# Macaron layer with mixture-of-experts on one Trainium2 core: routing weights leave the sorted rows, and the third pool is sorted in one part

## The reference

```
x = x + 0.5 * ffn(layernorm(x))
x = x + attention(layernorm(x))      # causal, 16 heads, 4 key/value heads, width 128, rotary embedding
x = x + 0.5 * ffn(layernorm(x))

def ffn(x):                          # 16 experts of width 96, the best 2 for each token
    probs = softmax(x @ router_w)
    w, idx = top_k(probs, 2);  w = w / sum(w)
    y[e] = (silu(x @ gate_w[e]) * (x @ up_w[e])) @ down_w[e]
    return sum over the two chosen experts of w * y[e]
```

## Time and profile before

| | us |
|---|---|
| median of 3 runs | 965.21 (961.5 to 966.19) |
| the profiled execution | 959.92, its span 958.1 |
| busy in the span: PE, DVE, ACT, POOL | 817.7, 653.4, 572.4, 449.1 |
| L1547 and L1554, scatters | 32 and 32 |
| L1573 and L1568, gathers | 32 and 32 |
| L1227, evacuations | 124 |

### The profile page before, as it was taken

One profiled execution on the slowest core, in us unless ns is written; L12 is line 12 of the kernel. 1 busy time (PEld: TensorE's weight loads), 2 busy tenths in 40 slices (PEclk: granted clock), 3 DMA queues, 4 the chain that ended last, 5 costly groups with the idle time before them and its releaser, 6 DMA issues.

```text
span 958.1 us, 16817 instructions
## 1 busy us (share of the span) xinstructions
PE 817.7 (85%) x4840; PEld 689.6 (72%) x4840; DVE 653.4 (68%) x1592; ACT 572.4 (60%) x1536; POOL 449.1 (47%) x410
## 2 busy tenths in 40 slices
PE   4648999798999999999999999999996958989480
PEld 3637877677878788787888888787775837768370
DVE  5814665477787778788878788867789836565153
ACT  3314756686777677776787776876664624445140
POOL 1571233486586667563564563544434570030623
PEclk9977999999999999999999999999999979999785
DMA  9356983211011102000000000000000452465544
GB/s 296 122 182 180 270 225 114 73 18 21 7 17 18 17 1 28 8 1 1 1 1 2 1 1 1 2 2 7 1 1 1 171 159 63 128 185 174 162 136 153
DMA packets 52952, 70.73 MB, mean 74 GB/s; under 512 B 7552, under 2 KB 44672, under 8 KB 52480
## 3 DMA queue, kind: packets, MB, share of 16 engines
q1 hardware_dynamic: 40768, 47.61, 16.2%
q0 software_dynamic: 9216, 16.82, 7.1%
q10 hardware_dynamic: 2880, 5.24, 1.8%
HBM read 42.61 MB, written 27.03 MB: 73 GB/s over the span
## 4 chain that ended last, share of the span: by engine, by line
PE 52%; issue 16%; POOL 13%; DVE 9%; DMA 4%; ACT 3%; another core or an unknown queue 2%; ACTq 0%; DVEq 0%; SPq 0%; POOLq 0%
PE ps L1637 43%; PE ps L1833 4%; POOL sb_x L1573 3%; POOL sb_ropeB L1582 3%; POOL sb_xf L1585 3%; PE ps L1691 2%; POOL sb_wF L1593 1%; POOL xs L1554 1%; DMA sb_x<-ys,sb_pos 1%; PE ps L1705 1%; DVE sb_x L1433 1%; DVE sb_nmax L1406 1%; DVE sb_wF L1413 1%; POOL xs L1547 1%
## 5 line engine op out<-in xcount | busy, mean ns | idle before, releaser
L1637 PE MATMUL ps<-sb_wF 128*128 128x512 f32 (+2 forms) x1056 | 283.4, 391 | 21.0 <-issue 9.2
L1637 PEld LDWEIGHTS ps<-sb_wF 128*128 128x128 f32 x1056 | 173.1, 195 | 35.6 <-issue 14.9
L1582 POOL TENSOR_TENSOR sb_ropeB<-sb_ropeB,sb_sin 128x512 f32<-128x512 f32 x80 | 109.5, 1369 | 147.7 <-ACT sb_ropeB L951 147.7
L971 ACT ACTIVATE sb_prob<-ps,sb_nmax 128x128 f32<-128x128 f32 (+3 forms) x256 | 134.3, 526 | 65.4 <-DVE sb_nmax L1406 61.7
L1637 PE MATMUL ps<-sb_wF,sb_wA 128*128 128x512 f32 x576 | 155.4, 405 | 7.1 <-ACT sb_ropeB L951 5.9
L1406 DVE TENSOR_REDUCE sb_nmax<-ps 128x1 f32<-128x128 f32 (+3 forms) x256 | 122.2, 485 | 55.7 <-PE ps L1637 49.3
L1593 POOL TENSOR_TENSOR sb_wF<-sb_xf,sb_wF 128x384 fp32r<-128x384 f32 (+1 forms) x75 | 85.5, 1140 | 119.2 <-ACT sb_wF L963 119.2
L1433 DVE SCALAR_TENSOR_TENSOR sb_x<-ps,sb_rinv,sb_x 128x256 f32<-128x256 f32 x256 | 122.7, 479 | 25.6 <-PE ps L1637 10.6
L1413 DVE TENSOR_TENSOR sb_wF<-ps,sb_wF 128x512 fp32r<-128x512 f32 x160 | 109.5, 684 | 34.3 <-ACT sb_wF L980 29.9
L1637 PE MATMUL ps<-sb_wA,sb_wF 128*128 128x256 f32 x768 | 118.5, 292 | 13.9 <-DVE sb_x L1433 13.7
L1637 PEld LDWEIGHTS ps<-sb_wA,sb_wF 128*128 128x128 f32 x768 | 109.5, 195 | 24.5 <-issue 16.6
(11 more groups left out here) (200 smaller groups left out, 1348.9 us busy)
## 6 DMA issues: line engine op xcount, KB each, us to landing
ys<-sb_wA_raw SPq DMA_DIRECT2D x124, 128.0 KB
sb_wF_raw<-xs SPq DMA_DIRECT2D x44, 128.5 KB
sb_wA_raw<-xs SPq DMA_DIRECT2D x44, 128.5 KB
sb_work<-xs SPq DMA_DIRECT2D x36, 128.5 KB
sb_wA_raw<-in_wattn ACTq DMA_DIRECT2D x18, 256.0 KB, 3.9
sb_wF_raw<-in_wgu SPq DMA_DIRECT2D x4, 768.0 KB, 10.0
sb_wF_raw<-in_wdn SPq DMA_DIRECT2D x4, 768.0 KB, 16.7
sb_wA_raw<-in_wgu SPq DMA_DIRECT2D x4, 768.0 KB
```

The lines of the kernel that those rows point to most:

```text
L971: nc.scalar.activation(prob[k % 2][:, h, 0:(i + 1) * P], ps[:, bank_of((k * G + h) % (UB * G)), 0:(i + 1) * P], ACT.Exp, bias=nmax[:, k % ...
L1582: nc.gpsimd.tensor_tensor(ropeB[:, slot], ropeB[:, slot], sin[:], ALU.mult).then_inc(rope_mul, 1)
L1637: return nc.tensor.matmul(out, lhsT, rhs, start=start, stop=stop)
```

## The change

Rows have 256 numbers. The weights of both choices stay in SBUF (`wgt` has two planes). Both scatters of a token tile are issued from the same untouched row, all first choices ahead of all second ones, with no copy and no wait between them. `evacuate` is a plain copy. `shares` comes after `places` in each pool. The first ffn's gathers become plain transfers into four slots (rows of pool 0 for the first 8, `work` for the others), and DVE adds each with `scalar_tensor_tensor` (x = y * weight + x), at places of its own in `first_norm` and in the groups; the same instruction takes the place of L1313 in the second ffn. The norm of batch 0 comes two steps later in `first_norm`. The third pool's routing is one part over 12 token tiles, its logits and choices stand in groups 0 and 1, its places in group 2, and of its 24 scatters 9 stand in POOL's group 2 and 15 at the head of group 3.

```diff
-    RW = D + 1
-    xs = [nc.dram_tensor(f"xs{n}", (pools[n].pairs + P, RW), F32) for n in range(2)]
+    xs = [nc.dram_tensor(f"xs{n}", (pools[n].pairs + P, D), F32) for n in range(2)]
-    RING, XR, FR, GR = 8, 10, 4, 16
+    RING, XR, AR, GR = 8, 10, 4, 16
-    LN_FIRST = {5: (0,), 6: (1,), 7: (2, 3), 9: (5, 6), 10: (7,)}
+    LN_FIRST = {6: (0,), 7: (1, 2), 8: (3,), 9: (5, 6), 10: (7,)}
-    GATHERS = {(0, 1): range(12, 16), (0, 2): range(16, 20), (0, 3): range(20, 26), (1, 1): range(26, 32)}
+    GATHERS = {(0, 1): range(12, 16), (0, 3): range(16, 20), (0, 4): range(20, 24), (1, 3): range(24, 28),
+               (1, 4): range(28, 32)}
+    RESULTS_AT = {1: (0.0, 0.3, 0.3, 0.5), 3: (0.25, 0.6, 0.6, 1.0), 4: (0.0, 0.4, 0.4, 0.9)}
...
-                items = spread(items, [("gather", 0, j) for j in GATHERS[b, g]], 0.0, 0.5 if g == 1 else 1.0)
+                items = spread(items, [("gather", 0, j) for j in GATHERS[b, g]], *RESULTS_AT[g][0:2])
+            if (b, g) in GATHERS and engine == "dve":
+                items = spread(items, [("result", 0, j) for j in GATHERS[b, g]], *RESULTS_AT[g][2:4])
...
-        "act": {0: [(0.05, 0.4, range(8))], 1: [(0.2, 0.4, range(12, 16))]},
-        "dve": {0: [(0.76, 0.86, range(2)), (0.9, 1.0, range(2, 4))],
-                1: [(0.04, 0.1, range(4, 6)), (0.4, 1.0, range(12, 18))],
-                2: [(0.02, 0.4, range(18, 25)), (0.7, 0.9, range(26, 29))]},
-        "pool": {3: [(0.0, 0.0, range(12 + SECOND))]},
+        "act": {0: [(0.05, 0.4, range(8))], 1: [(0.0, 0.2, range(12, 16))]},
+        "dve": {0: [(0.7, 0.76, range(2)), (0.78, 0.82, range(2, 4)), (0.92, 0.96, range(4, 6))],
+                1: [(0.52, 0.98, range(12, 19))], 2: [(0.22, 0.5, range(20, 24))]},
+        "pool": {2: [(0.3, 1.0, range(9))], 3: [(0.0, 0.0, range(9, 2 * MT))]},
...
         def shares(q):
             dve.wait_ge(gtanh_done, q.p + 1)
-            tanh = gap(q, 1)
-            step(nc.vector.tensor_scalar(row_weights(q), tanh, 0.25, 0.25, ALU.mult, ALU.add))
-            nc.vector.tensor_scalar(wgt[:, q.t0:q.t0 + q.nt], tanh, -0.25, 0.25, ALU.mult, ALU.add)\
-              .then_inc(weight_done, 1)
-            settle()
+            for k, half in enumerate((0.25, -0.25)):
+                link(nc.vector.tensor_scalar(wgt[:, k, q.t0:q.t0 + q.nt], gap(q, 1), half, 0.25, ALU.mult, ALU.add))
+
+        def weighted_add(t, k, y):
+            return nc.vector.scalar_tensor_tensor(x[:, t // T, t % T], y, wgt[:, k, t:t + 1], x[:, t // T, t % T], ALU.mult,
+                                                  ALU.add)
+        def result(j):
+            t, k = pair(0, j)
+            dve.wait_ge(res_in[j % AR], 16 * (j // AR + 1))
+            if k == 1:
+                dve.wait_ge(res_done, j)
+            weighted_add(t, k, result_at(j)).then_inc(res_done, 1)
...
-            nc.vector.tensor_scalar(yo(s), y_at(s), tile_at(q, s)[:, D:D + 1], None, ALU.mult).then_inc(y_evac, 1)
+            nc.vector.tensor_copy(yo(s), y_at(s)).then_inc(y_evac, 1)
...
         def first_norm(i):
-            if 12 <= i < 12 + T:
-                dve.wait_ge(acc_in[i - 12], accumulated(1))
+            if 6 <= i < 6 + 2 * T:
+                result(i - 6)
+            if 14 <= i < 14 + T:
+                dve.wait_ge(res_done, T + i - 13)
...
-            elif i in (20, 21):
+            elif i in (21, 22):
...
-            elif n < 18:
-                chosen[q.p] = (0, 2 * T)
+            elif n < 19:
                 route(q, n - 12)
-                del chosen[q.p]
-            elif n < 24:
-                chosen[q.p] = (2 * T, q.nt)
-                route(q, n - 18)
-                del chosen[q.p]
...
         def scatter(q, n):
-            at = q.tokens + n
+            k, t = divmod(n, q.nt)
             if n == 0:
-                pool.wait_ge(weight_done, q.p + 1)
                 pool.wait_ge(to_done, q.p + 1)
...
+            nc.gpsimd.indirect_dma_start(out=xs[q.p][:], out_offset=place_of(q, k, t), in_=row(q, t),
+                                         in_offset=None).then_inc(scattered[q.p], 16)
...
-            nc.gpsimd.indirect_dma_start(out=x[:, t // T, t % T], out_offset=None, in_=ys[q.p][:], in_offset=where,
-                                         compute_op=ALU.add).then_inc(acc_in[t], 16)
+            if j >= AR:
+                pool.wait_ge(res_done, j - AR + 1)
+            if j % (2 * T) == 0 and j >= 4 * T:
+                pool.wait_ge(proj_done, normed(j // (2 * T) - 1))
+            nc.gpsimd.indirect_dma_start(out=result_at(j), out_offset=None, in_=ys[q.p][:],
+                                         in_offset=where).then_inc(res_in[j % AR], 16)
...
-        do(0, head_of("dve"))
+        do(0, spread(head_of("dve"), [("result", 0, j) for j in range(2 * T, 3 * T)], 0.5, 1.0))
```

More of the change, by code:

```diff
@@ L111, in program @@
         C = routing(own, "C")
-        rowC = sb("rowC", [P, MT, RW], F32, own)
+        rowC = sb("rowC", [P, MT, D], F32, own)
         C.update(placing(own, "C"))
@@ L213, in program @@
     y_out = [sem(f"y_out{r}") for r in range(RING)]
-    acc_in = [sem(f"acc_in{t}") for t in range(N)]
+    res_in = [sem(f"res_in{r}") for r in range(AR)]
+    res_done = sem("res_done")
     gat_in = [sem(f"gat_in{r}") for r in range(GR)]
@@ L352, in counts_of, with normed @@
         return counts or [JB[i] * b + v for i, v in enumerate(task_count(k, col))]
+    def normed(b):
+        n = max(n for n, (k, c) in enumerate(order) if c < 0)
+        return G + 3 + (b - 1) * JB[0] + n + 1
     def values_use(g):
@@ L437, in tile_at @@
         if r >= 7:
-            return work[:, (r - 7) * RW:(r - 6) * RW]
+            return work[:, (r - 7) * D:(r - 6) * D]
         flat, base = ((wF_flat, 20 * 512), (wA_flat, 27 * 512))[q.n]
-        return flat[:, base + r * RW:base + (r + 1) * RW]
+        return flat[:, base + r * D:base + (r + 1) * D]
     def rows_of(q):
@@ L593, in turn_of @@
                 items = third_pool(engine, g - KV, items)
+                if engine == "pool":
+                    items = spread(items, [("power", 0, 2 * B)], 0.8, 0.85)
             out += items
         return out
-    SECOND = 3
     EARLY_ROWS = 8
@@ L706, in gathers_of, with result_at @@
         return range(2 * q.t0, 2 * (q.t0 + q.nt))
-    def accumulated(k):
-        return 16 * (k + 1)
+    def result_at(j):
+        return (row(pools[0], j % AR) if j < 2 * T else work[:, (j % AR) * D:(j % AR + 1) * D])
     ADD_FROM = 7
@@ L1278, in last_pool @@
                 route(q, i - 10)
-            elif i == 18:
+            elif 18 <= i < 23:
+                places(q, i - 18)
+            elif i == 23:
                 shares(q)
-                places(q, 0)
-            elif 19 <= i < 23:
-                places(q, i - 18)
         def experts(n):
@@ L1312, in gather_add @@
                 dve.wait_ge(gadd_done, j)
-            nc.vector.tensor_tensor(xs_t, xs_t, gathered(j), ALU.add).then_inc(gadd_done, 1)
+            weighted_add(t, k, gathered(j)).then_inc(gadd_done, 1)
         def third(n):
@@ L1455, in do @@
                     early_norm(k, n)
+                elif what == "result":
+                    result(n)
                 elif n < 2:
                     if n == 0:
-                        for t in range(T):
-                            dve.wait_ge(acc_in[(b + 1) * T + t], accumulated(1))
+                        dve.wait_ge(res_done, 2 * T * (b + 2))
                     norm_stats(stats, b + 1, 2 * n, 2 * n)
@@ L1505, in _ @@
             route(pools[0], part)
-        shares(pools[0])
         for part in range(5):
             places(pools[0], part)
+        shares(pools[0])
         second_choices(0, 2 * FIRST_HALVES)
@@ L1511, in _ @@
         route(pools[1], 6)
-        shares(pools[1])
         for part in range(5):
             places(pools[1], part)
+        shares(pools[1])
         experts(0)
-        do(0, head_of("dve"))
+        do(0, spread(head_of("dve"), [("result", 0, j) for j in range(2 * T, 3 * T)], 0.5, 1.0))
         for b in range(B - 1):
@@ L1613, in _ @@
         for q in pools[0:2]:
-            for n in range(q.nt + SECOND):
+            for n in range(2 * q.nt):
                 scatter(q, n)
@@ L1626, in _ @@
         power(*NORMS[2 * B + 1])
-        for n in range(pools[3].nt + SECOND):
+        for n in range(2 * pools[3].nt):
             scatter(pools[3], n)
```

60 lines of the change are left out of this document (18 added, 42 removed), and 12 rows, old and new, of the table AFTER.

## The result

| | before | after |
|---|---|---|
| median of 12 runs | 964.90 us | 959.16 us |
| lowest, highest | 959.66, 967.16 | 956.17, 963.15 |
| ratio | | 0.9953 (0.9931 to 0.9974) |
| profiled execution, its span | 959.92, 958.1 | 963.15, 961.3 |

The medians lie 5.7 us apart; the ratio puts the gain at 4.5 us (2.5 to 6.7 by the interval). I forecast 12.4.

What follows compares the result with a forecast made beforehand. PE was taken to bound most of attention, with losses under POOL's transfer bursts and in pool 2's sort. Terms -2 + 0 + 3 - 2 - 11.4 = -12.4 took 959.9 to 947.5, 952.8 in the median's terms; range 940 to 969.

Steps and rivals of the forecast that it cites:

- pool 2's scatters: Last attention group: 15 scatters replace 34 transfers, the burst's first 14 us free of slowing; -11.4 us, bounds 0 and -14.3.
- The freeze: In PE's three low stretches, POOL's dense indirect transfers, beside SP's, slow instruction starts on other engines; 14.3 us between 768 and 792.
- Scatters of pools 0 and 1: At the start: shorter bursts without copies, first tile 0.9 us sooner, pool 1 2 us sooner; -2 us, bounds -3 and +2.
- First eight gathers: First norm: plain gathers save a 3.0 us wait, DVE's additions cost it back; sum 0, bounds -3 and +5.
- Additions in attention: 24 DVE additions at 0.69, 16.6 us, a fifth let through; +3 us, bounds 0 and 35.
- B: Rival: DVE's additions in attention are held by POOL's rope instructions, +5.6 us in all, about 971; chance 0.13.
- Sort of pool 2: Attention groups: routing in one part takes 2.2 us less DVE, group 1 +3, group 2 -5; sum -2, bounds -10 and +5.
- Sort and scatters together: Third pool's routing in attention and its scatters in the last group: terms of -2 and -11.4 us.
- Second ffn: Pool 3's scatters save a us, 32 additions gain an operand, the gather burst is untouched; 0.
- A: Rival: last group's slowing stays, belonging to the down weights or any burst meeting them; about 964; chance 0.18.
- D: Rival: the eight plain gathers of the first norm bring a freeze of their own; +5, about 958; chance 0.07.
- C: Rival: more goes, burst over before the freeze, group 2 at 38, DVE free for additions; -22.4, about 943; chance 0.12.

Runs made afterwards that it cites:

- e1: Changed kernel with pool 2's last 15 scatters issued one for each row maximum of the last group; 943.76 us, 0.9793 of the kernel before.
- e7: Changed kernel with gate, up and down weights asked for only after pool 2's scatters have landed; 957.41 us, 0.9922 of the kernel before.
- e12: As e14, but the 15 scatters at the head of the last group, each followed by a 192-column product on POOL; 913.80 us, 0.9536.
- e15: Changed kernel once more, unedited, on one chip beside the old sort; 956.55 us, 0.9986 of the kernel before.
- e2: Changed kernel with pool 2's 24 gathers in the second ffn issued one for each evacuated tile; 945.15 us, 0.9784 of the kernel before.
- e8: Changed kernel with pool 2's last 15 scatters in three rows of five; 951.27 us, 0.9849 of the kernel before.
- c2: Changed kernel run again with no edit; 0.9941 of the kernel before, span 961.0.
- e10: As e14, with each weighted addition in attention made in two DVE steps; 935.52 us, 0.9698 of the kernel before.
- e16: Repeat of e6 beside the changed kernel on one chip; 971.28 us, 1.0145 of the kernel before.
- e13: Changed kernel with the old sort, the three rows broken up, pool 2's 24 scatters over the last group's 16 maxima; 927.02 us, 0.9690.
- e14: Changed kernel with pool 1's scatters, pool 2's last 15 scatters and pool 2's gathers all broken up; 912.04 us, 0.9544 of the kernel before.
- e6: Changed kernel with the third pool sorted as before and all 24 plain scatters heading the last group; 970.22 us, 1.0113 of the kernel before.
- e9: As e14, with pool 3's 8 scatters also issued one for each expert tile; 912.16 us, 0.9456 of the kernel before.
- e3: Changed kernel with pool 1's scatters issued one for each expert tile after the first four; 941.46 us, 0.9834 of the kernel before.

## Why the prediction was right or wrong

**The step that failed** is the one on pool 2's scatters: "The first 14 us of a burst were free of it there. Of the 19 us 5 are left, at 14.3 / 24 = 0.6 us lost for each: 3. So -11.4". The freeze itself was read rightly (e1, e7, e12), its onset wrongly. 14 us held for one row with a pause in it; "The burst itself runs on evenly" was said from its first and its last scatter, and it doesn't. In the changed kernel's row the freeze begins after 7.5 us, six scatters. So 12 of the 19 us are frozen, and at not 0.6 but 15 / 12 = 1.2 us each: by e1's two windows PE is idle 10 us more in the group and busy 5 us longer, at the lower clock after its standstill. The last group went from 47.9 and 51.2 to 48.0 and 47.3: some -2. That its true length is 33 us I could have had from the earlier trace rows: 34.9 for a group with projections, and the last has none.

**Scatters of pools 0 and 1, -2 (bounds -3 and +2).** The bursts are 10.1 and 30.0 us long, as I said. But the 21st tile comes at 103.7 and 104.7 in the place of 100.9 and 100.7: +3 to +4, past my bound, though it isn't the same in every execution (e15's is 100.5, and those of e1, e2, e7 and e8 are 102.6 to 103.2). "A denser burst may let fewer tiles through" was the right doubt, and it needed a price: PE stands still for 15.8 us in one piece, against 6.3 at the longest before. The first tile is 2.7 us later, although its rows are sorted 2 us sooner: DVE makes its product only after pool 1's places, and these ended at 50.1, 2.2 later.

**First eight gathers, 0.** From the 21st tile to the end of group 1 +2.9, within the bounds. The first addition waits 4.2 us for its row (3.2 in c2), where the norm had waited 3.0.

**Additions in attention, +3.** Their durations are those of L1077, as I chose: median 0.75, longest 1.50, 19.2 us in sum against my 16.6. Groups 2 to 12 became 2.9 us shorter. The step that was off is the fifth that I let through: for the net it was below nothing, for a further operation (e10) it is eight tenths. The Trainium skill, "SBUF — State Buffer", section "SBUF: two separate sides", names the lock under which one such operation waits for POOL's; the lengths agree (0.45 to 1.50 us beside POOL's operations of 1.3), and B's conclusion from them doesn't.

**Sort of pool 2, -2.** The markers of groups 1 and 2 of batch 3 are 42.6 and 43.6 us apart, where I had 49 and 42. Group 0, which I had left alone, grew by 3 to 4 us (43.3 and 42.8 before; 46.0 in c2 and 47.6, from the marker at 619.7 to the one at 667.3), in which more of the sort now stands. Together the three lost 2 to 3 us: the sum was right, its places weren't.

**Sort and scatters together** I had at -13.4: measured -14.7 on one chip and -15.0 with the rows broken up. All the rest at +1: measured +14.1 with the rows as they are, 0 with them broken up. The agreement of the first pair is luck: -14.7 is counted from e16, whose last group the unbroken row had made 58 us long, and not from the kernel before; -15.0 is counted from e13, whose last group was still 40. So the sum failed where I didn't look, in what plain scatters do to the density of a row.

**Second ffn, 0.** 160.4 and 160.7 against 157.8 and 161.2.

**The rivals.** A came out as to the number, for another reason than its own: the weights have at most 2 of its 15 us (e7). By the same section of the Trainium skill, neither side of SBUF slows the other, and no scatter could stop ACT or PE. The runs show scatters that do, at one distance and not at another; which part of the chip carries it they don't show. D named a freeze by the eight gathers: PE does stand still for 3.5 us beside them, but behind DVE, which waits 4.2 us for its first row. That is a wait for data, and no run shows a freeze there. B and C didn't happen. The range held the time; "faster by over 0.5%" had 0.71, and the result lies on that border (0.9953, and 0.9941 in c2).

## What to carry to other kernels

In this kernel indirect transfers of POOL in an unbroken row are paid by all engines, not by POOL: count how many follow one another without a pause, and put a wait or some 0.6 us of other work between them (a copy of 0.18 us was not enough here). Three such rows cost the changed kernel some 44 us (956.6 in e15, 912.0 in e14, each on a chip where before takes 957), about eight times what the change itself gained at best. A wait that looks like waste may be the pause that keeps a row harmless; before it is removed, ask what becomes denser. And a price per us "after the first 14" needs the timeline between the first and the last row, not those two.

## What the runs showed of the hardware

- Plain indirect transfers of 128 rows of 1 KB, each 0.96 us on POOL and 0.30 apart: after 7.5 us of a row of 15 in attention (six of them; the changed kernel, c2, e7, e15) and 9.2 and 9.4 us of a row of 24 (e16, e6), ACT, DVE and PE start little until the row ends: PE is busy 0.14 of six us at the worst. Beside expert tiles PE's first gap over 3 us begins 4.9 to 8.9 us after the first of pool 2's gathers, and PE is busy 9 to 11 of 24 us. ACT's longest gap in a row of scatters was 8.8 (e15) to 12.9 us (e16). With 0.6 us of other POOL work between them (1.9 us from one to the next, e12) there is no gap over 1.7 us on PE. Which part of the chip carries it stays open. All these executions had their span and clock recorded, so no run shows whether the recording has a part in it.
- It needs no other transfer: between 757.0 and 770.6 of e7 no other packet moves, of data or of instructions. And 283 GB/s of plain loads alone leave PE busy 96%.
- A row of five costs 1.5 us on average (e8), one of eight 2.5 to 6 by its own stretch (e9), one of 15 some 15 (e1), one of 24 some 26 in attention (e6, 58.9 - 32.7) and some 20 at the start (e3).
- PE's granted clock was lower where it stood still and just after: 0.68 over 15 us of e7, where PE was busy 5.0 us, 0.55 in the four us after six idle ones in the changed kernel, and 1.00 over the same group with the row broken up (e1).
- The kernel before takes 957 us on two chips and 965 on two, more than the change is worth.
